# Transposing the later halves of x on VectorE instead of TensorE, from a second load by 32 by 32 blocks

## The reference, cut to what matters

```
x: [128, 32, 256], q = relu(cond @ W3 + b3)          # one row of q for each of 128 batches
v = (32 * x + sum of x over the 32 positions) * q      # q is the same for all positions of a batch
c = relu(v @ W2 + b2)                                  # [4096, 256]
w1q, w3q, w2q = ternary(w1), ternary(w3), ternary(w2)  # signs times one scale, zero below half the mean size
g = silu(c @ w1q.T) * (c @ w3q.T)                      # hidden width 682
out = x + g @ w2q.T
```

## Time and profile before

| | |
|---|---|
| median of three runs | 176.47 us |
| profiled execution | 176.39 us |
| its span, first to last instruction | 174.2 us |
| TensorE matmuls busy | 169.4 us (97%) |
| VectorE busy | 103.1 us (59%) |
| ScalarE busy | 87.0 us (50%) |
| GpSimd busy | 34.6 us (20%) |
| granted TensorE clock | 0.998 of full speed |

### The profile page before, as it was taken

The page is one execution under the profiler, slowest core; times in us unless marked ns, Lnnn a source line. Parts: engine busy times, 40 slices in busy tenths (PEclk is TensorE's granted clock), DMA queues, the critical chain, the costliest instruction groups (busy, mean ns, idle before and its releaser), DMA issues.

```text
span 174.2 us, 2563 instructions
## 1 busy us (share of the span) xinstructions
PE 169.4 (97%) x966; PEld 145.4 (83%) x966; DVE 103.1 (59%) x170; ACT 87.0 (50%) x161; POOL 34.6 (20%) x38
## 2 busy tenths in 40 slices
PE   7999999999999999999999999999999999999993
PEld 2988777888888888888889888888889888988792
DVE  2339939654864279353874369443874439456763
ACT  4169873645543372555534282554535285254640
POOL 5000005710505050320605041230605020000000
PEclk9999999999999999999999999999999999999999
DMA  4999082000030003000030003000030003000303
GB/s 141 311 360 349 32 268 93 0 4 4 0 120 0 4 0 120 0 0 4 0 120 0 0 4 109 11 0 0 4 120 0 0 4 120 4 0 0 120 4 120
DMA packets 10901, 11.11 MB, mean 64 GB/s; under 512 B 561, under 2 KB 10633, under 8 KB 10889
## 3 DMA queue, kind: packets, MB, share of 16 engines
q1 hardware_dynamic: 10600, 10.75, 18.8%
q10 hardware_dynamic: 288, 0.20, 0.4%
HBM read 6.75 MB, written 4.19 MB: 63 GB/s over the span
## 4 chain that ended last, share of the span: by engine, by line
PE 90%; DVE 3%; DMA 2%; SPq 1%; ACT 1%; POOL 1%; issue 0%; POOLq 0%; ACTq 0%
PE bank L461 46%; PE bank L490 24%; PE bank L391 15%; PE bank L365 3%; DMA xo<-in_x_dram 2%; DVE w_t L581 2%; PE bank L377 1%; POOL x L228 1%; PE bank L415 0%; DVE x L545 0%; DVE vsum L550 0%; DVE y L557 0%; ACT silu L323 0%; ACT T L284 0%; DVE xo L648 0%
## 5 line engine op out<-in xcount | busy, mean ns | idle before, releaser
L461 PE MATMUL bank<-c_hi,T 128*128 128x512 f32 (+1 forms) x176 | 71.1, 404 | 0.2 <-ACT T L288 0.2
L461 PE MATMUL bank<-c_lo,T 128*128 128x512 f32 (+1 forms) x176 | 69.5, 395 | 0.0
L323 ACT ACTIVATE silu<-bank,checked 128x512 f32<-128x512 f32 (+1 forms) x48 | 33.0, 688 | 72.1 <-PE bank L461 72.1
L635 DVE TENSOR_TENSOR gf<-silu,bank 128x512 f32<-128x512 f32 (+1 forms) x48 | 32.9, 685 | 53.4 <-PE bank L461 44.7
L461 PEld LDWEIGHTS bank<-c_hi,T 128*128 128x128 f32 (+1 forms) x176 | 32.8, 186 | 6.8 <-ACT T L288 0.6
L461 PEld LDWEIGHTS bank<-c_lo,T 128*128 128x128 f32 (+1 forms) x176 | 32.8, 187 | 6.2
L490 PE MATMUL bank<-T,g_hi 128*128 128x256 f32 x160 | 34.1, 291 | 0.0
L233 POOL TENSOR_TENSOR c_lo<-ct,c_hi 128x512 fp32r<-128x512 f32 x12 | 17.6, 1470 | 82.1 <-ACT c_hi L274 82.1
L490 PE MATMUL bank<-T,g_lo 128*128 128x256 f32 x160 | 32.6, 281 | 0.0
L391 PE MATMUL bank<-x,W_sb 128*128 128x256 f32 x128 | 30.5, 381 | 0.5 <-POOL x L228 0.4
L642 DVE TENSOR_TENSOR g_lo<-gf,g_hi 128x512 fp32r<-128x512 f32 x40 | 29.0, 724 | 1.2 <-ACT g_hi L330 1.2
(11 more groups left out here) (61 smaller groups left out, 82.4 us busy)
## 6 DMA issues: line engine op xcount, KB each, us to landing
out_dram<-xo SPq DMA_DIRECT2D x15, 256.0 KB, 2.2
xo<-in_x_dram SPq DMA_DIRECT2D x6, 512.0 KB, 7.3
w_sb<-in_L_ffn_w_dram SPq DMA_DIRECT2D x2, 640.0 KB
xo<-in_x_dram SPq DMA_DIRECT2D x4, 256.0 KB, 4.8
w_sb<-in_L_ffn_w_dram SPq DMA_DIRECT2D x1, 682.0 KB, 8.0
W_sb<-in_L_cond_W_dram SPq DMA_DIRECT2D x1, 256.0 KB, 3.9
out_dram<-xo SPq DMA_DIRECT2D x2, 128.0 KB, 2.1
W_sb<-in_L_cond_W_dram ACTq DMA_DIRECT2D x1, 128.0 KB, 2.5
```

The lines of the kernel that those rows point to most:

```text
L323: nc.scalar.activation(silu[r, m % 2, :], h1[j % 2][r], ACT.Silu, scale=checked[r, 0:1]).then_inc(silu_done, 1)
L461: last = pe.matmul(dst[j % 2][0:w, :], T13[:, k, col:col + w], part[:, g, k, :], start=(i == 0), stop=(i == len(passes) - 1))
L635: nc.vector.tensor_tensor(gf[r, m % 3, :], silu[r, m % 2, :], second, ALU.mult).then_inc(g_done, 1)
```

## The change

The later halves (4 to 15) are no longer transposed by TensorE. SP loads x a second time into a new buffer `xb`, laid out so that each 32 by 32 block of x (32 positions of one batch, 32 channels) lies on the 32 partitions that the block's transpose shall have: four DMAs for each half, one for each quarter of the partitions, each of 512 runs of 128 bytes. VectorE then transposes a whole half in one instruction, block by block, from SBUF into a new SBUF buffer `xT` with two places. Sum and y read `xT`. On VectorE the sum now stands behind the low part of the step before. `xb` holds four halves; the loads of halves 4 to 7 stand on SP's queue behind w2 and ahead of groups 2 to 7 of x, those of halves 8 to 15 among the stores, each waiting for the transpose of the half four before it. TensorE's early halves keep their matmuls. `c_hi` and `c_lo` have room for four groups instead of eight and are used in turn.

```diff
+    x_b = x.rearrange("b s d -> (b s) d").rearrange("(n b t) (c q e) -> n q t c b e", b=HTB, t=BT, c=DC, e=BT)
...
+        xb = sb("xb", [P, EARLY, DC, HTB, BT], F32)
+        xT = sb("xT", [P, 2, DC, HT], F32)
...
-        c_hi = sb("c_hi", [P, NG, DC, GT], F32R)
-        c_lo = sb("c_lo", [P, NG, DC, GT], F32R)
+        c_hi = sb("c_hi", [P, NC, DC, GT], F32R)
+        c_lo = sb("c_lo", [P, NC, DC, GT], F32R)
...
+            def load_blocks(n):
+                for q in range(QB):
+                    sp.dma_start(xb[q * BT:(q + 1) * BT, n % EARLY], x_b[n, q]).then_inc(got_blocks[n % EARLY], 16)
+
+            for n in range(EARLY, 2 * EARLY):
+                load_blocks(n)
             for g in range(AHEAD, NG):
...
             for g in range(NG - 1):
+                for n in range((g + 2 * AHEAD) * HALVES, min((g + 2 * AHEAD + 1) * HALVES, NH)):
+
+                    sp.wait_ge(xT_done, n - 2 * EARLY + 1)
+                    load_blocks(n)
                 for b in range(TT // 2):
...
-            def transpose_x(n):
-                pe.wait_ge(got_half[n] if n < EARLY else got_group[n // HALVES - AHEAD], 16)
-                bank_of_x_free(n)
-                xT = xT_of(n)
-                for c in range(DC):
-                    for t in range(HTT):
-                        col = c * HT + t * P
-                        last = pe.transpose(xT[:, col:col + P],
-                                            xo[:, n // HALVES, n % HALVES * HTT + t, c * P:(c + 1) * P], ident[:])
-                last.then_inc(xT_done, 1)
...
-                    last = pe.matmul(dst[j % 2][0:w, :], T13[:, k, col:col + w], part[:, g, k, :],
+                    last = pe.matmul(dst[j % 2][0:w, :], T13[:, k, col:col + w], part[:, g % NC, k, :],
...
-                n = half_at(m, (0, 2))
-                if n is not None:
-                    transpose_x(n)
                 n = half_at(m, (2, 5))
                 if n is not None:
                     project_c(n)
...
+            def transpose_x(n):
+                dve.wait_ge(got_blocks[n % EARLY], 16 * QB * (n // EARLY))
+                if n >= EARLY + 2:
+
+                    dve.wait_ge(y_done, n - EARLY - 1)
+                nc.vector.transpose(flat(xT[:, n % 2]), xb[:, n % EARLY].rearrange("p c b e -> p (c b e)")
+                                    ).then_inc(xT_done, 1)
...
                 n = half_at(m, (0, 2)) if m < NG * STEPS else None
                 if n is not None:
-                    sum_sequence(n)
+                    transpose_x(n)
                 if m:
                     lo_step(m - 1)
+                if n is not None:
+                    sum_sequence(n)
```

More of the change, by code:

```diff
@@ L40, in adaln_ternary_ffn_kernel @@
     NCT = 4
+    NC = 4
+    BT = 32
+    QB = P // BT
+    HTB = HT // BT
     W_COUNT = float(H * D)
-    assert B == P and Q == P and HR <= HR2 and RM <= P and NG == 8 and HT % S == 0 and DC == 2 and STEPS == 6 and EARLY == 4
+    assert B == P and Q == P and HR <= HR2 and RM <= P and NG == 8 and HT % S == 0 and DC == 2 and STEPS == 6 and EARLY == 4 and S == BT
     x_v = x.rearrange("b s d -> (b s) d").rearrange("(g t p) d -> g p t d", t=TT, p=P)
+    x_b = x.rearrange("b s d -> (b s) d").rearrange("(n b t) (c q e) -> n q t c b e", b=HTB, t=BT, c=DC, e=BT)
     out_v = out.rearrange("b s d -> (b s) d").rearrange("(g t p) d -> g p t d", t=TT, p=P)
@@ L117, in adaln_ternary_ffn_kernel, with mixed_of @@
         w2_ps = [bank[:, 4 + b, :].bitcast(BF16) for b in range(2)]
-        def xT_of(n):
-            return bank[:, 0 if n < EARLY and n % 2 else 6, :]
+        def mixed_of(n):
+            return bank[:, 0 if n % 2 else 6, :]
         def z_of(n):
@@ L127, in adaln_ternary_ffn_kernel @@
         got_half = [sem(f"got_half{n}") for n in range(EARLY)]
+        got_blocks = [sem(f"got_blocks{n}") for n in range(EARLY)]
         got_group = [sem(f"got_group{g}") for g in range(AHEAD, NG)]
@@ L143, in adaln_ternary_ffn_kernel @@
         T1_copied, T3_copied, T2_copied = sem("T1_copied"), sem("T3_copied"), sem("T2_copied")
-        xT_done, vsum_done, y_done, x1_done = sem("xT_done"), sem("vsum_done"), sem("y_done"), sem("x1_done")
+        mixed_done, xT_done, vsum_done, y_done, x1_done = sem("mixed_done"), sem("xT_done"), sem("vsum_done"), sem("y_done"), sem("x1_done")
         z_done, relu_done, c_hi_done, c_lo_done = sem("z_done"), sem("relu_done"), sem("c_hi_done"), sem("c_lo_done")
@@ L162, in half_of @@
         def half_of(tensor, n):
-            return tensor[:, n // HALVES, :, n % HALVES * HT:(n % HALVES + 1) * HT]
+            return tensor[:, n // HALVES % NC, :, n % HALVES * HT:(n % HALVES + 1) * HT]
         def rows_of(j):
@@ L350, in _, with mix_x @@
         def _(pe):
[L351 to L355, removed]
+            def mix_x(n):
+                pe.wait_ge(got_half[n], 16)
+                if n >= 2:
                     pe.wait_ge(x1_done, n - 1)
-            def transpose_x(n):
-                pe.wait_ge(got_half[n] if n < EARLY else got_group[n // HALVES - AHEAD], 16)
-                bank_of_x_free(n)
-                xT = xT_of(n)
+                mixed = mixed_of(n)
                 for c in range(DC):
@@ L364, in transpose_x @@
                         col = c * HT + t * P
-                        last = pe.transpose(xT[:, col:col + P],
-                                            xo[:, n // HALVES, n % HALVES * HTT + t, c * P:(c + 1) * P], ident[:])
-                last.then_inc(xT_done, 1)
[L369 to L373, removed]
-                for c in range(DC):
-                    for t in range(HTT):
-                        col = c * HT + t * P
-                        last = pe.matmul(xT[:, col:col + P],
+                        last = pe.matmul(mixed[:, col:col + P],
                                          xo[:, n // HALVES, n % HALVES * HTT + t, c * P:(c + 1) * P], mix[:],
                                          start=True, stop=True)
-                last.then_inc(xT_done, 1)
+                last.then_inc(mixed_done, 1)
             def project_c(n):
@@ L543, in scale_mixed @@
             def scale_mixed(n):
-                dve.wait_ge(xT_done, n + 1)
-                nc.vector.tensor_tensor(by_batch(flat(x1[:, n % 2])), by_batch(xT_of(n)),
+                dve.wait_ge(mixed_done, n + 1)
+                nc.vector.tensor_tensor(by_batch(flat(x1[:, n % 2])), by_batch(mixed_of(n)),
                                         over_sequence(flat(qT[:, n])), ALU.mult).then_inc(x1_done, 1)
+            def transpose_x(n):
[4 more added lines that the diff above has]
+                                    ).then_inc(xT_done, 1)
             def sum_sequence(n):
-                dve.wait_ge(xT_done, n + 1)
-                nc.vector.tensor_reduce(vsum[:, n % 2, :], by_batch(xT_of(n)), AX.X, ALU.add).then_inc(vsum_done, 1)
+                dve.wait_ge(xT_done, n - EARLY + 1)
+                nc.vector.tensor_reduce(vsum[:, n % 2, :], by_batch(flat(xT[:, n % 2])), AX.X, ALU.add).then_inc(vsum_done, 1)
             def add_sum(n):
@@ L557, in add_sum @@
                 nc.vector.scalar_tensor_tensor(
-                    out=by_batch(flat(y[:, n % 2])), in0=by_batch(xT_of(n)), scalar=float(S),
+                    out=by_batch(flat(y[:, n % 2])), in0=by_batch(flat(xT[:, n % 2])), scalar=float(S),
                     in1=over_sequence(vsum[:, n % 2, :]), op0=ALU.mult, op1=ALU.add).then_inc(y_done, 1)
```

## The result

The changed kernel takes 171.6 us (median of four runs, 171.47 to 172.13) against 176.47: a ratio of 0.974, 95% interval 0.971 to 0.976. The forecast was 171.1, range 170.4 to 174.4. The profiled execution takes 171.47 us, 4.92 less than the one of before.

A forecast was written before the change was run, and what follows sets the result against it. TensorE, 97% busy and without idle time in the steady part, was taken as the bound. From the profiled 176.39 us, less 5.83 of transposes and wait, plus 0.5 of new waiting: 171.06, forecast 171.1 us, range 170.4 to 174.4.

The forecast's parts named there:

- The gain on TensorE: Steady steps j=0 and j=2: removing TensorE's transposes saves 0.43 + 0.44 us in each of five groups, 4.35.
- The start: First group, halves 4 and 5: 0.49 us of transposes and a 0.99 wait for GpSimd's product both go.
- The wait that comes back: Even half's projection: TensorE waits for GpSimd's product because y comes later; 0.1 us in each of five groups, 0.5 in all.
- the slack of 0.3 us: Even half: GpSimd's product ends at 85.90, TensorE reaches the projection at 86.21; a collision slowing y may use it up.
- VectorE's transpose: VectorE gains 12 transposes of 128x512 fp32, taken as 0.68 us each; bounds 0.41 and 1.36, another estimate 1.24.
- The block loads: 48 more loads on SP's queue, 39 ns a packet: half 4 lands at 20.6, in time; cost 0.
- my doubled price: Block loads at twice queue 1's price per packet, should read-modify-write double it: half 7 lands at 65.8, time 190 us.
- TensorE's time was given back: Denies a rival, chance 0.06: another wait sets TensorE's pace, some 0.35 us of each of 12 halves returns as idle, 174.8.
- The late blocks: Rival, chance 0.11: block loads land late, VectorE's transposes hold up TensorE; gain gone from 66 ns a packet, 178.8 at 75.
- The late chain: Rival, chance 0.12: transpose costs 1.36 us, TensorE waits 0.4 to 0.8 at the even half's projection; 173.9 us.
- The odd half: Step j=2: y ends 1.4 us later but its product stands behind other GpSimd work; nothing charged, uncovered up to 0.7 per group.
- the rings: c's parts in rings of four groups: same instructions on other addresses, no wait added; cost 0.

The follow-up runs named there:

- e1: Changed kernel without VectorE's transposes, sum and y reading the loaded blocks untransposed (output not the reference's): 170.42 us, ratio 0.967.
- e10: Changed kernel unaltered, run again on the same chip as a version with two repairs: 171.39 us, ratio 0.971.
- e7: Changed kernel with the block loads of halves 4 to 7 behind all loads of x on SP's queue: 180.77 us, ratio 1.023.
- e4: Changed kernel with every VectorE transpose done twice, the second into a buffer nobody reads: 177.55 us, ratio 1.007.
- e2: Changed kernel with each even half's transpose, from half 6 on, moved one step earlier to the end of j=5: 170.51 us, ratio 0.967.
- e5: Kernel before the change with only c's parts put in rings of four groups: 176.63 us, ratio 0.999.
- e6: e5 plus the 48 block loads, waited for by VectorE but read by nobody, TensorE still transposing: 181.64 us, ratio 1.029.

## Why the prediction was right

**The gain on TensorE** was predicted as 0.43 + 0.44 a group; e1 gives 19.83 - 18.94 = 0.89. Reading starts rather than durations was what made it right: four transposes show 0.60 us in one row and cost 0.35, and the 0.08 behind them is seen only in the next matmul's start.

**The start**: predicted 1.48, found 1.31. The wait of 0.39 and its 0.6 of transposes are gone, as said; but this execution began its hidden products 0.19 later (18.79 against 18.60), and e10, which began at 18.53, has its second group at 38.13, 1.56 earlier than before. From the first group's first product to the second's it is 19.43 us after and 20.93 before, 1.50 less. The term was right; the 0.19 is within the spread of the starts, though its cause isn't shown.

**The wait that comes back** is the term of the sum that was mis-sized: 0.1 us a group allowed, 0.16 found (19.10 less 18.94), five times 0.06 = 0.3 us. The 0.1 was an allowance, set above the 0.05 that the count gave, so part of the nearness is luck. Its place and its cause were right: the product of the even half at the projection, through a y that starts later and collides with c_lo. The count for y was near: its start slipped 0.75 (from 4.19 to 4.94 after the group's first product) and not 0.68, and the collision cost 0.26 of at most 0.36. What was wrong is the slack of 0.3 us, taken up to the projection's first matmul: the weight load needs x up to 0.20 us sooner, and its late start is the 0.10 us that come on top of the wait. With the 0.19 of the start, and less the 0.02 a group that the transposes were worth above my reading, this is the distance of 0.4 to the profiled 171.47.

**VectorE's transpose**: 0.68 predicted, 0.703 found. The estimate of 1.24 us was too high: the figure in the Trainium skill, "VectorE: DVE Perf Modes", section "The three transpose paths", is 311 ns for one 128x128 transpose of bf16. Scaling it by four does not hold here: four fp32 pieces in one instruction take 0.70.

**The block loads**: in time, as said, but on a wrong price. 39 ns a packet was predicted and 13 found; half 4 landed at 16.7 where 20.6 was forecast and 22.0 needed. Behind the earlier loads the rate was set by SP, at 0.68 us a DMA where I had 1.24. Had the packet term decided anything, its nearest row would have misled by a factor of three; only the bounds were safe. The row of queue 10 was a mixture: packet by packet, the trace of the kernel before has a median of 27 ns for 512 bytes and 46 ns for 1 KB. The line through these two gives some 13 ns for 128 bytes, the median found. The rule of 512 bytes for line rate in the Trainium skill, "DMA: Bandwidth & Descriptors", section "Specifications", asks for 512 B or more. As to the rate it fits: 16 engines with one packet of 128 bytes every 13 ns would move nearly 160 GB/s, an estimate from that median, where the large loads reach 310 to 360 on the page. As to the read-modify-write that it names below 512 B, these loads show nothing: 98 ns, my doubled price, is far off, and 13 ns lies on the line of the larger packets. It is still twice the 6 ns by bytes alone, which that line puts down to a cost of some 8 ns per packet of any size.

**The rivals.** TensorE's time was given back, 0.89 us a group in e1. The late blocks were priced well as a wait (e7) and too low as time, since the clock was left out, 2.6 us of it. The late chain was priced badly: 173.9 for a transpose of 1.36 us, and e4 gave 177.55 for 1.37. The step that fails is "the low part, for which TensorE waits, stays where it is". It holds for one transpose because the low part starts 0.14 us before c_lo; with two it starts behind it, takes 1.38 instead of 0.69, and a second wait opens ahead of the one that I watched. **The odd half** (nothing charged) and **the rings** (0) are confirmed: e2 keeps the odd halves' transposes and has the period of e1 without them, 18.94, and e5 shows no change.

## What to carry to other kernels

Work moved from the bound engine to one with idle time is free only up to the slack of the next chain through it; compute that slack up to the start of what reads the result, which for a matmul's weights is the weight load and not the matmul, and keep a step in reserve: here moving the transpose into an idle stretch brought the period from 19.10 to 18.94, a further 0.8 us over five groups. A load with a new place in a queue has to be judged by everything behind it, and by whether its reader is still the same: the same 16 loads cost nothing in one kernel and 5 us in the other. When you double a suspected cost as a test, look where the wait appears; it need not be on the chain that you suspect.

## What the runs showed of the hardware

A VectorE operation with two SBUF operands and a GpSimd operation nearly queue: the one that starts second ends late by the overlap less some 0.14 us. c_lo takes 1.29 us alone, 1.71 when VectorE's low part started 0.14 before it (overlap 0.55), and 1.30 when it was first and the low part took 1.38 instead of 0.69 (e4, overlap 0.84). Operations with a single SBUF operand kept their time beside c_lo: the sum 0.69 in the changed kernel, the second transpose 0.67 in e4, and y 0.69 in the kernel before, where its other operand was in PSUM. The Trainium skill, "SBUF — State Buffer", section "Who interferes with whom", says that a VectorE instruction with two SBUF inputs contends with a GpSimd instruction that reads SBUF, and that the order of issue decides who blocks; this case agrees. I had used an average slowdown; by the order of the two, the larger part of e4's cost could have been foreseen.

A projection's first weight load overlaps the matmul before it by 0.20 us when its operand is there. When it isn't, the first matmul starts with the load and takes 0.32 to the next start instead of 0.21.

DMA packets have medians of 13 ns for 128 bytes, 27 for 512 and 46 for 1 KB on a DMA engine. A DMA of 512 runs of 128 bytes holds SP for 0.63 us (median of 48), and for up to 2.67 while larger loads are under way (the eight issued from 28.78 on took 11.32 us).

After 4 to 7.5 us without work TensorE ran with a granted clock of 0.50 for the next 5 us of work (e6, e7).
